# A Mamba block with a top-2 mixture of experts: order of ScalarE's copies and of the loads in the front, two buffers for second weights and another PSUM bank for the last sums

## The reference

```python
xn  = layernorm(x)
# 1. a state-space layer, inner width 256
xp, z   = split(xn @ W_in.T)                     # 2 x 256
xc      = silu(causal_conv4(xp) + conv_b)        # 4 taps, per channel
Bm, Cm, dt_in = split(xc @ W_x.T)                # 16, 16, 256
dt      = softplus(dt_in @ W_dt.T + b_dt)
alpha   = clip(sigmoid(0.1 * dt), .01, .99)
h[t]    = alpha * h[t-1] + (1 - alpha) * sigmoid(mean(Bm)) * xc
attn    = ((h * sigmoid(mean(Cm)) + D * xc) * silu(z)) @ W_out.T
# 2. experts: 8, hidden width 256, the best 2 of each token
logits  = xn @ w_gate ; top 2, softmax over the two
ffn     = sum_k p_k * (silu(xn @ w1[e_k]) * (xn @ w3[e_k])) @ w2[e_k]
out     = x + attn + ffn
```

## Time and profile before

| | us |
|---|---|
| median of 3 runs | 471.16 (471.15 to 471.25) |
| the profiled execution's own time | 471.31 |
| its span in the trace | 469.6 |
| TensorE busy | 430.6 (92%) |
| VectorE busy | 388.1 (83%) |
| GpSimd busy | 310.6 (66%) |
| ScalarE busy | 287.7 (61%) |

### The profile page before, as it was taken

How to read it: one execution, slowest core, us unless ns; L and a number is a source line. 1 busy time by engine, 2 the same in 40 slices (tenths; PEclk the granted TensorE clock), 3 DMA queues, 4 the chain that set the end, 5 groups by cost and what they waited for, 6 DMA issues and landing times.

```text
span 469.6 us, 8332 instructions
## 1 busy us (share of the span) xinstructions
PE 430.6 (92%) x2440; PEld 308.0 (66%) x2440; DVE 388.1 (83%) x774; ACT 287.7 (61%) x406; POOL 310.6 (66%) x344
## 2 busy tenths in 40 slices
PE   0888999999999999998999999999999878998877
PEld 0777544555554455555888888988988878664446
DVE  5885897999999999996998997677677675399985
ACT  2774469788888988898454434434434433668850
POOL 4677777777777775750677777777777777764200
PEclk9998999999999999999999999999999999999999
DMA  8961117131121312143677756666656652029994
GB/s 239 292 195 45 53 52 239 46 98 54 56 88 52 97 50 82 47 136 98 201 202 239 224 172 198 187 184 177 175 170 190 182 143 85 15 46 266 209 211 121
DMA packets 48077, 65.92 MB, mean 140 GB/s; under 512 B 8424, under 2 KB 30223, under 8 KB 48048
## 3 DMA queue, kind: packets, MB, share of 16 engines
q1 hardware_dynamic: 36240, 39.56, 30.2%
q0 software_dynamic: 10656, 24.47, 18.6%
q10 hardware_dynamic: 1152, 1.57, 1.2%
HBM read 42.09 MB, written 33.83 MB: 162 GB/s over the span
## 4 chain that ended last, share of the span: by engine, by line
PE 48%; DVE 29%; issue 13%; ACT 8%; DMA 1%; DVEq 0%; SPq 0%; ACTq 0%
PE PD L897 13%; DVE hbuf L1404 6%; PE PB L729 4%; DVE hbuf L1415 4%; PE PD L840 3%; PE PB L859 3%; PE PB L863 3%; PE PB L860 3%; PE PA L859 3%; DVE gbuf L1386 3%; PE PA L863 3%; PE PA L860 3%; DVE y L1424 2%; DVE gbuf L1292 2%; PE PC L744 2%
## 5 line engine op out<-in xcount | busy, mean ns | idle before, releaser
L612 POOL DMA_INDIRECT moe_out<-xnT,dst_u x142 | 146.6, 1033 | 61.7 <-issue 37.8
L597 POOL DMA_INDIRECT moe_in<-xn,slot_u x128 | 133.0, 1039 | 44.4 <-issue 39.9
L897 PE MATMUL PD<-xnT,xn 128*128 128x128 f32 x536 | 66.0, 276 | 1.3 <-DVE xn L1630 1.2
L897 PEld LDWEIGHTS PD<-xnT,xn 128*128 128x128 f32 x536 | 62.7, 192 | 2.4 <-DVE xn L1630 2.0
L744 PE MATMUL PC<-xc,Wc 128*128 128x512 f32 x128 | 57.8, 594 | 2.9 <-ACT xc L1102 2.9
L1176 ACT ACTIVATE whi<-xnT 128x512 fp32r<-128x512 f32 x36 | 22.8, 633 | 61.3 <-PE PB L863 61.3
L1205 ACT ACTIVATE xn<-PA 128x1024 f32<-128x1024 f32 (+1 forms) x36 | 36.5, 1013 | 34.4 <-PE PA L863 20.2
L757 PE MATMUL PA<-xnT,Wtap 128*128 (+4 forms) x128 | 57.2, 590 | 0.0
L1630 DVE TENSOR_TENSOR xn<-xn,PB 128x1024 f32<-128x1024 f32 (+1 forms) x36 | 43.4, 1207 | 11.1 <-PE PB L863 9.0
L1623 DVE TENSOR_TENSOR xlo<-PD,xhi 128x512 fp32r<-128x512 f32 (+1 forms) x36 | 24.6, 682 | 27.6 <-ACT xhi L1199 27.6
L757 PEld LDWEIGHTS PA<-xnT,Wtap 128*128 128x128 f32 x128 | 24.3, 190 | 30.5 <-issue 30.5
(11 more groups left out here) (246 smaller groups left out, 916.9 us busy)
## 6 DMA issues: line engine op xcount, KB each, us to landing
xnT<-moe_w SPq DMA_DIRECT2D x36, 256.0 KB
xn<-moe_in SPq DMA_DIRECT2D x31, 266.0 KB
out_dram<-moe_out POOLq DMA_DIRECT2D x12, 512.0 KB, 16.3
xnT<-moe_w SPq DMA_DIRECT2D x36, 128.0 KB
out_dram<-xacc SPq DMA_DIRECT2D x7, 512.0 KB, 3.5
moe_out<-xnT,dst_u POOLq DMA_INDIRECT x142
moe_in<-zrow SPq DMA_DIRECT2D x8, 266.0 KB, 3.4
moe_w<-in_L_ffn_w_dram SPq DMA_DIRECT2D x2, 1024.0 KB
```

The lines of the kernel that those rows point to most:

```text
L597: gp.indirect_dma_start(xs_dram, bass.IndirectOffsetOnAxis(ap=slot_u[:, k, j:j + 1], axis=0), xn_row[:, j, :], None).then_inc(s_scat, 16)
L612: gp.indirect_dma_start(yt_dram, bass.IndirectOffsetOnAxis(ap=dst_u[:, t, j:j + 1], axis=0), yo[t % OUTS][:, j, :], None, bounds_check=lim ...
L897: last = pe.matmul(PD[:, 512 + j * D:512 + (j + 1) * D], hid[b][:, k * SLOTS + j * P:k * SLOTS + (j + 1) * P], (w2x[t - FULL] if mixed and ...
```

## The change

Front: VectorE normalises group 15 as well (ROWS_V), behind group 13; ScalarE's normalise(15) goes. ScalarE does take(10) before root(3), and take(11) before normalise(12). SP loads x's last quarter behind the ten weight loads. Mixed tiles: whix and wlox get two buffers, taken in turn; ScalarE and VectorE wait only for the product of the mixed tile two before, and low_mixed comes ahead of the GLU. End: last_rows and the out sums for add_out(16) go to PC instead of PB, TensorE waits for the last softplus (which reads PC) there and for add_out(15) only before the last group's sums; the eight unread products go; VectorE's add_out(16) reads PC and comes behind parts 3 and 5 of the chain.

```diff
-ROWS_V = (13,)
+ROWS_V = (13, 15)
...
-        whix = sb("whix", [P, 2 * HID], F32R)
-        wlox = sb("wlox", [P, 2 * HID], F32R)
+        whix = sb("whix", [P, 2, 2 * HID], F32R)
+        wlox = sb("wlox", [P, 2, 2 * HID], F32R)
...
-            for q in range(QUARTERS):
-                if q == 0:
...
+            sp.dma_start(wg[:, :], w_gate).then_inc(s_wg, 16)
+            for q in range(1, QUARTERS - 1):
+                sp.dma_start(xacc[:, q * QT:(q + 1) * QT, :], x_q[q]).then_inc(s_x[q], 16)
             sp.dma_start(win_raw, W_in.rearrange("(a p) h -> p a h", p=P)).then_inc(s_wld, 16)
...
             sp.dma_start(dsk[:, :], D_skip.rearrange("(c p) -> p c", p=P)).then_inc(s_wld, 16)
+            sp.dma_start(xacc[:, (QUARTERS - 1) * QT:TILES, :], x_q[QUARTERS - 1]).then_inc(s_x[QUARTERS - 1], 16)
             sp.dma_start(wp_dram[:, :, 0:HID], w1).then_inc(s_pack, 16)
...
-                hi, lo = (whi[:, b, :], whix[:, :]), (wlo[:, b, :], wlox[:, :])
+                x = max(t - FULL, 0) % 2
+                hi, lo = (whi[:, b, :], whix[:, x, :]), (wlo[:, b, :], wlox[:, x, :])
...
             out(g, g % SLOT3, True)
-            pe.wait_ge(s_add, g)
             pe.wait_ge(s_rows, 16 * TOP_K)
-            pe.matmul(PB[:, 0:GROUP], ident[:, :], last_rows[0][:, 0:GROUP], start=True, stop=False)
-            pe.matmul(PB[:, 0:GROUP], ident[:, :], last_rows[1][:, 0:GROUP], start=False, stop=False)
+            pe.wait_ge(s_dt, GROUPS)
+            for c in range(TOP_K):
+                pe.matmul(PC[:, 0:GROUP], ident[:, :], last_rows[c][:, 0:GROUP], start=(c == 0), stop=False)
             pe.wait_ge(s_y2, g)
...
-            pe.wait_ge(s_ch, (GROUPS - 1) * CHAIN + 5)
-            for _ in range(8):
-                pe.matmul(PC[:, 0:P], ident[:, :], ident[:, :], start=True, stop=True)
-            pe.wait_ge(s_add, GROUPS)
+            pe.wait_ge(s_add, g)
...
             take(8)
             take(9)
+            take(10)
             root(3)
-            take(10)
             setup(3)
+            take(11)
             normalise(12)
-            take(11)
             take(12)
-            normalise(15)
             take(13)
...
                 act.wait_ge(s_w13x[m], 16)
-                if m:
-                    act.wait_ge(s_h3, t)
-                act.activation(whix[:, :], w13x[m], ACT.Copy).then_inc(s_whix, 1)
+                if m > 1:
+                    act.wait_ge(s_h3, t - 1)
+                act.activation(whix[:, m % 2, :], w13x[m], ACT.Copy).then_inc(s_whix, 1)
...
             scale(13)
+            scale(15)
...
-                ve.wait_ge(s_whix, t - FULL + 1)
-                if t > FULL:
-                    ve.wait_ge(s_h3, t)
+                m = t - FULL
+                ve.wait_ge(s_whix, m + 1)
+                if m > 1:
+                    ve.wait_ge(s_h3, t - 1)
...
-                glu(t, b, early)
                 if isinstance(t, int) and is_mixed(t + 1):
                     low_mixed(t + 1, 1 - b)
+                glu(t, b, early)
...
             chain(g, slot, 2)
-            add_out(g)
             chain(g, slot, 3)
             chain(g, slot, 5)
+            add_out(g, 0, PC)
```

More of the change, by code:

```diff
@@ L373, in _ @@
         def _(sp):
-            for q in range(QUARTERS):
-                if q == 0:
[L376 to L381, removed]
+            sp.dma_start(xacc[:, 0:QT // 2, :], x_q[0][:, 0:QT // 2]).then_inc(s_x0, 16)
+            sp.dma_start(xacc[:, QT // 2:QT, :], x_q[0][:, QT // 2:QT]).then_inc(s_x[0], 16)
+            sp.dma_start(wg[:, :], w_gate).then_inc(s_wg, 16)
+            for q in range(1, QUARTERS - 1):
+                sp.dma_start(xacc[:, q * QT:(q + 1) * QT, :], x_q[q]).then_inc(s_x[q], 16)
             sp.dma_start(win_raw, W_in.rearrange("(a p) h -> p a h", p=P)).then_inc(s_wld, 16)
@@ L968, in _ @@
                 for k in range(HALVES):
-                    last = pe.matmul(PB[:, j * D:(j + 1) * D], gated_y(g)[:, k, j * P:(j + 1) * P], WoT[:, k, :],
+                    last = pe.matmul(PC[:, j * D:(j + 1) * D], gated_y(g)[:, k, j * P:(j + 1) * P], WoT[:, k, :],
                                      start=False, stop=(j == GT - 1 and k == HALVES - 1))
             last.then_inc(s_out, 1)
-            pe.wait_ge(s_ch, (GROUPS - 1) * CHAIN + 5)
-            for _ in range(8):
-                pe.matmul(PC[:, 0:P], ident[:, :], ident[:, :], start=True, stop=True)
-            pe.wait_ge(s_add, GROUPS)
+            pe.wait_ge(s_add, g)
             for h in range(2):
@@ L1493, in tap, with add_out @@
                                         a_v, ALU.mult, ALU.add).then_inc(s_taps if j == TAPS - 1 else s_cv, 1)
-            def add_out(g, col=0):
+            def add_out(g, col=0, ps=PB):
                 static = isinstance(g, int)
@@ L1501, in add_out @@
                 at = bass.ds(g * GT - 2 * GT, GT) if not static else slice((g - 2) * GT, (g - 1) * GT)
-                ve.tensor_tensor(xacc[:, at, :], PB[:, col:col + GROUP].rearrange("p (j d) -> p j d", j=GT),
+                ve.tensor_tensor(xacc[:, at, :], ps[:, col:col + GROUP].rearrange("p (j d) -> p j d", j=GT),
                                  xacc[:, at, :], ALU.add).then_inc(s_add, 1)
@@ L1641, in low_mixed @@
             def low_mixed(t, b):
-                ve.wait_ge(s_whix, t - FULL + 1)
-                if t > FULL:
-                    ve.wait_ge(s_h3, t)
-                ve.tensor_tensor(wlox[:, :], w13x[t - FULL], whix[:, :].bitcast(F32), ALU.subtract).then_inc(s_wlox, 1)
+                m = t - FULL
+                ve.wait_ge(s_whix, m + 1)
+                if m > 1:
+                    ve.wait_ge(s_h3, t - 1)
+                ve.tensor_tensor(wlox[:, m % 2, :], w13x[m], whix[:, m % 2, :].bitcast(F32), ALU.subtract).then_inc(s_wlox, 1)
             def match(t, n, b, first):
```

## The result

The changed kernel takes 466.22 us (median of 4 runs, 465.56 to 466.42), the kernel before beside it 471.21 (4 runs); the ratio is 0.9893, 95% interval 0.9879 to 0.9907. It is 5.0 us faster where 8.3 were forecast, and outside the range given. The profiled execution took 466.38 us with a span of 464.6, against 471.31 and 469.6.

The account below looks back on a forecast made before the run. It took a chain of waits as the bound: the scatters' own rate in front, TensorE in the tiles, the last sums at the end. Gains 1.7 + 5.8 + 0.8 = 8.3 us gave 462.9 us; 8-in-10 range 460.4 to 465.4.

Parts of the forecast that it names:

- End, DMA: Kernel's end: sums by DMA end at about 459, 8.6 us before the span, binding only if the rest gains over 10.
- Mixed tiles: Tiles 31 to 34: two buffers remove TensorE's wait for wlox, 1.45 us a tile, 5.8 in all; bounds 4.8 and 5.8.
- Front: Before tile 0: ScalarE's new order lets tile 0's transposes start at 212.0, held by their load; 1.7 us, bounds 0.4 and 3.4.
- allowance of 1.3 us for the end of the scatters: Front: with VectorE shifted against GpSimd, the end of the row scatters may move by 1.3 us either way.
- Weights' order: Front: x's last quarter loaded behind the weights ends TensorE's 0.98 us wait, but ScalarE takes the gain; 0 counted.
- Last sums: Last group: VectorE 2.6 us sooner, half clock under the last 16 matmuls costs 1.8; gain 0.8, bounds 0.8 and 2.6.
- 1: Rival, more arrives: the scatters' gap closes or the clock stays up at the end; 461.1 us, chance 0.20.
- 2: Rival: scatters hold the front or its half clock stays, 0.4 there, mixed tiles 4.8; 465.2 us, chance 0.15.
- 3: Rival, front: x's last quarter lands L us late, time 462.9 + L, up to 473.6 us; chance 0.04.
- 5: Rival, no change: gains cancel against more of rival 3, with L between 8 and 9; chance 0.02.
- 4: Rival, end: last stores take turns with the sums by DMA and land 2 us later; 464.9 us, chance 0.10.
- the window 423 to 424: Earlier trace: sums' queue moved 1 packet, stores' queue 601, read as a store being hardly held up by the sums.

Follow-up runs that it names:

- e1: The changed kernel with GpSimd's last three waits, for the sums by DMA, moved to the end of SyncE's list: 462.93 us.
- h2: The kernel before with the mixed tiles' two buffers and the three waits for the sums moved to SyncE: 465.21 us.
- e2: The kernel before with GpSimd's last three waits for the sums by DMA moved to SyncE: 471.11 us, no change.
- g4: e1 with the whole front put back (x's last quarter ahead of the weights, ScalarE's old order, normalise(15) on ScalarE): 464.43 us.
- e4: e1 with 28 identity products before the wait for the last y, to keep the clock up: 463.59 us.
- h3: e1 with 12 identity products ahead of the last y: 462.93 us.
- k1: e1 with the last sums put back (old bank, wait for the add, eight identity products): 464.13 us.
- e3: The changed kernel with 28 identity products before the wait for the last y, to keep the clock up: 466.84 us.
- k2: e1 with x's last quarter loaded ahead of the weights again: 463.21 us.
- k3: e1 with ScalarE's old order in the front and normalise(15) on ScalarE: 465.36 us.
- h1: The kernel before with the mixed tiles' two buffers only: 467.82 us.
- f1: Same kernel as h1, in a session where the kernel before took 562.09 us: ratio 0.9929.
- f3: The changed kernel without the mixed tiles' two buffers, in the session where the kernel before took 562.09 us: ratio 0.9982; not run again.
- f2: Same kernel as h2, in the session where the kernel before took 562.09 us: ratio 0.9863.
- f4: Same kernel as h3, in the session where the kernel before took 562.09 us: ratio 0.9854.

## Why the prediction was wrong

**The step that failed** is "End, DMA": that the sums by DMA "end at about 459" and "become the bound only if the rest gains over 10 us". The first half held: the last landing was seen at 458.5. But behind the landing GpSimd has a drain of 5.63 us, and with it they became the bound as soon as the rest gained 4.9. The row stood in the trace of the kernel before (461.8, 5628 ns) and I had not looked behind the last packet: I measured the slack of a transfer to the end of the span, not that of the engine that waits for it. The work of the other engines came 7.6 us sooner, but 2.7 us of it were lost to the drain.

With the waits moved (e1) the time is 462.93, where 462.9 was forecast. That is partly luck. In e1's profiled execution (462.07 us) the last matmuls start 10.6 us sooner than before, not 8.3: 2.3 in the front, 5.7 in the mixed tiles and 2.6 in the last group, with no half clock behind it. Then 1.3 us are lost because the last store lands 3.1 us behind its issue instead of 1.8. The other steps, one by one:

- **Mixed tiles**, 5.8 forecast: right. The trace has 5.7 (down products in tile 34 sooner by 6.8, of which 1.1 came with the front), h2 against e2 5.9.
- **Front**, 1.7 (0.4 to 3.4): the size is within the bounds (1.5 by g4), and the mechanism held: a half clock gone, tile 0 waiting for its load. The profiled execution showed only 1.1, since its first scatter was issued at 32.0, not at 30.6 "as before". e1, which has the same front, issued it at 30.8 and had tile 0 at 211.40, 2.3 us sooner than before; so the delay was no part of the change (last section). The allowance of 1.3 us for the end of the scatters was right: tile 0 follows the first scatter by 180.6 us in after, e1, e4, h3 and k1, and by 181.9 to 182.0 in e3 and k2.
- **Weights' order**, 0: right within 0.3 (k2), with ScalarE's new order. With the old one g4 and k3 are 0.9 us apart, for a reason that is open.
- **Last sums**, 2.6 - 1.8 = 0.8: both numbers in the trace. y was ready 9.4 us sooner, 6.8 of it passed on and 2.6 new; the 16 matmuls took 3.79 for 2.05, so 1.7 went back. But the 2.6 was read from an execution in which the clock had fallen before L964. VectorE's wait of 2.02 us there was mostly this: in h1, h2 and k1 the old code ran at full clock at this place, and the same wait is 0.34. The row of h2:

```profile
453.08 0.69 DVE L1503 TENSOR_TENSOR xacc<-PB,xacc 128x512 f32<-128x512 f32 x1 [0.34 <-PE PB L970]
```

  From the start of out(15) to the start of the last 16 matmuls it is 13.4 us in the kernel before, 11.7 in h1, h2 and k1, and 10.8 in after and e1. Against the old code at full clock the edit is worth 0.9 us. As k1 measured it, it is 1.2, not clear of the noise.
- **Rivals.** 1 and 2 didn't come. 3 didn't: no wait for x's last quarter. The time came out slower than all of them but 3 and 5. 4 was not the cause in after, but its mechanism is real. I had read the earlier trace rows wrongly: the window 423 to 424 does not show the two queues at work together. The first sum had just ended (0.53 MB moved), and the next three, though issued from 418.38 on, moved nothing until 424.2; why they paused is not shown. From 426 to 433 of the kernel before both queues moved packets all the time, and about one for one:

```profile
q0 software_dynamic: 272, 0.98, 70.4%
q1 hardware_dynamic: 266, 0.94, 35.9%
```

  From 453 to 454 of after the rows are

```profile
q0 software_dynamic: 52, 0.18, 92.4%
q1 hardware_dynamic: 55, 0.03, 13.5%
```

  One small packet of the stores for one large packet of the sums: the turns of the rule that the prediction quoted from the Trainium skill (DMA: Bandwidth & Descriptors, Queues, rings and completion order). These windows agree with it, and my row did not bear against it. But turns are not all of it: the 512 KB store issued at 448.5 moves no packet at all before 452, while q0 moves 55 to 63 a microsecond, and no run shows why. Then it crawls at 0.02 to 0.03 MB a microsecond until the sums end, and takes 10.4 us to land, where its like took 7.6 in the earlier trace rows. Its rest stands ahead of the last stores. In after this hides under the half clock. In h3 SyncE's side ends at 460.9, 0.7 us behind GpSimd's drain: q1 has 2 us of full traffic behind the sums' end, and a faster TensorE brought nothing in the median. In 457 to 458 of h3, the sums gone:

```profile
q1 hardware_dynamic: 675, 0.34, 111.8%
```

  Then the end is set by the sums' start and the bytes behind them. This last reading is argued from the traces; no kernel with fewer bytes was run.

## What to carry to other kernels

When an engine's last act is to wait for transfers, its work ends where its closing drain ends, not where the last byte lands: look up every engine's last instruction in the trace before an end is called free. Let the engine with the cheap close (SyncE, 13 ns here) wait for transfers and let the one with the dear close (GpSimd, 5.63 us) run out early; e1 did this and is the fastest kernel of the study with h3, 462.93 us. Do not take the drain for hidden then: in e1 it still ended last by 0.1 us. When a wait is read from a trace as the gain of an edit, look at the granted clock under it: here 1.7 of 2.0 us were the clock's. And before two queues are said not to hinder each other, take a window in which both have work.

## What the runs showed of the hardware

- **GpSimd's drain** took 5628 ns, to the nanosecond, in before, after, e3, f1, f3 and h1, where it began behind the landings, and 18.0 to 18.6 us in e1, e2, e4, f2, f4, g4, h2, h3 and k1 to k3, where it began behind the last issue.
- **How long the first matmuls run slow differs between executions.** TensorE starts at 12.1 to 12.3 us everywhere. Its first matmuls take twice as long as later ones, until 15.4 us in the kernel before and 18.7 in e2, whose program differs only at its end. This looks like the half clock, but the trace doesn't show it as such: the granted clock of these windows reads 1.00. The eight logits at 14.2 us in after and in before:

```profile
14.22 2.08 PE L674 MATMUL PC<-wg,xnT 128*128 128x128 f32 x8
```

```profile
14.19 1.72 PE L676 MATMUL PC<-wg,xnT 128*128 128x128 f32 x8
```

  The first scatter follows it: 30.6 us where the slow part ends at 15.4 (before), 30.8 at about 15.4 (e1), 31.3 at about 16.3 (e4), 32.0 at about 17.3 (after) and 32.1 at 18.7 (e2, the old front). A front must be compared at equal starts, or over many executions.
- **The same idle time costs the clock or not.** TensorE stood idle 3.58 us before its last 16 matmuls in after and 3.57 in e1; they took 3.79 us in after and 2.05 in e1:

```profile
454.16 2.05 PE L982 MATMUL PB<-WoT,y 128*128 128x128 f32 x16 [3.57 <-DVE y L1423]
```

  I had taken the fall as certain. It differs between executions, and what decides it is open: in after all four runs have a mean granted clock of 0.988 or 0.989, in e1 none of five is below 0.992. It goes with part of the 1 to 2 us by which runs of one kernel differ. Of the 17 runs of the kernel before beside e1, the five with a mean clock of 0.993 took 471.3 to 471.4 us, the five at 1.0 took 469.9 to 471.1.
